# A recurrent mixing block: rel on GpSimd from an SBUF logarithm, nine hidden chunks on VectorE, the first sequence in halves, loads and all engine orders changed

## What is computed

```python
xn = layernorm(x)
shifted = pad(xn)[:, :-1]                       # one token later
k = (xn * mk + shifted * (1 - mk)) @ Wk         # v, r alike
r = sigmoid(r)
# for each token, per channel: num, den, mx carried on
out = (e1 * num + e2 * v) / (e1 * den + e2)     # with running maximum mx
s = (r * out) @ Wo
h = relu(xn @ w1[0] + b1[0])                    # 128 -> 512
z = layernorm(xn + h @ w2[0] + b2[0]) * gamma + beta
result = x + s * silu(z)
```

## Time and profile before

| | us |
|---|---|
| median of 3 runs | 112.2 (111.92 to 112.39) |
| span of the profiled execution | 110.7 |
| TensorE, VectorE, ScalarE, GpSimd busy in it | 101.9, 96.0, 94.3, 66.0 |

### The profile page before, as it was taken

The page is one execution under the profiler, slowest core; times in us unless marked ns, Lnnn a source line. Parts: engine busy times, 40 slices in busy tenths (PEclk is TensorE's granted clock), DMA queues, the critical chain, the costliest instruction groups (busy, mean ns, idle before and its releaser), DMA issues. The chain is left out here.

```text
span 110.7 us, 1604 instructions
## 1 busy us (share of the span) xinstructions
PE 101.9 (92%) x336; PEld 56.7 (51%) x336; DVE 96.0 (87%) x199; ACT 94.3 (85%) x155; POOL 66.0 (60%) x104
## 2 busy tenths in 40 slices
PE   4997799997999999999999999999999999999660
PEld 4993335553465445553675553674554566435230
DVE  1647989979999999799988989999999897899980
ACT  1425087899999998999899999999999999999940
POOL 3009998986746469459999998743819403360000
PEclk9999999999999999999999999999999999999998
DMA  3999200000000000000002110000000002203134
...
DMA packets 9450, 5.09 MB, mean 46 GB/s; under 512 B 481, under 2 KB 9185, under 8 KB 9441
## 3 DMA queue, kind: packets, MB, share of 16 engines
...
q10 hardware_dynamic: 560, 0.40, 1.3%
...
## 5 line engine op out<-in xcount | busy, mean ns | idle before, releaser
L638 PE MATMUL bank<-hid,w_c 128*128 128x512 f32 x64 | 31.1, 592 | 0.0
L589 PE MATMUL bank<-mixed,w_in 128*128 128x512 f32 x48 | 24.1, 599 | 0.8 <-POOL mixed L379 0.7
L475 ACT ACTIVATE hid<-bank,vec 128x512 f32<-128x512 f32 x32 | 21.4, 683 | 1.1 <-PE bank L611 0.7
L716 DVE SCALAR_TENSOR_TENSOR mixed<-step_x,vec,bank 128x511 f32<-128x511 f32 x24 | 17.5, 738 | 1.6 <-POOL step_x L370 1.6
L638 PEld LDWEIGHTS bank<-hid,w_c 128*128 128x128 f32 x64 | 11.9, 190 | 10.8 <-issue 9.3
L609 PE MATMUL bank<-xT_hi,w_hi 128*128 128x512 f32 x28 | 15.5, 552 | 1.1 <-POOL xT_lo L361 1.1
L589 PEld LDWEIGHTS bank<-mixed,w_in 128*128 128x128 f32 x48 | 8.4, 189 | 10.1 <-issue 8.6
L370 POOL TENSOR_TENSOR step_x<-xT 128x512 f32<-128x512 f32 x8 | 8.3, 1037 | 8.5 <-ACT xT L467 8.4
L403 POOL TENSOR_TENSOR dv<-v_sb 128x512 f32<-128x512 f32 x8 | 9.8, 1227 | 5.8 <-ACT v_sb L526 5.8
L340 POOL TENSOR_SCALAR xn<-x_sb,neg_mean,rstd 128x128 f32<-128x128 f32 x28 | 12.2, 449 | 0.0
L755 DVE TENSOR_TENSOR_SCAN dev<-keep,dv 128x512 f32<-128x512 f32 x8 | 9.8, 1220 | 1.7 <-issue 0.8
...
## 6 DMA issues: line engine op xcount, KB each, us to landing
x_sb<-x SPq DMA_DIRECT2D x7, 256.0 KB, 6.6
block_out<-res SPq DMA_DIRECT2D x7, 256.0 KB, 2.3
w_in<-squares SPq DMA_DIRECT2D x1, 256.0 KB, 3.0
w_in<-w ACTq DMA_DIRECT2D x1, 256.0 KB, 5.4
w_in<-w SPq DMA_DIRECT2D x1, 256.0 KB, 6.3
...
```

Source lines behind the costliest of these rows:

```text
L475: act.activation(hid[b % 2][:, f, :], ps(f"up{f}", b)[:, :], ACT.Relu, bias=vec[:, B1_COLUMN + f:B1_COLUMN + f + 1]).then_inc(done[f"hid{f ...
L589: pe.matmul(ps(name, b)[:, :], w_in[:, which, :], mixed[b % 2][:, which, :], start=True, stop=True).then_inc(done[name], 1)
L638: pe.matmul(ps("z", b)[:, :], w2_c[:, f, :], hid[b % 2][:, f, :], start=False, stop=chunks_of(b)[-1] == f"z{f}", skip_group_check=True).th ...
L716: dve.scalar_tensor_tensor(mixed[n][:, which, 1:], step_x[n][:, 1:], vec[:, which:which + 1], ps("z", b)[:, 0:T - 1], ALU.mult, ALU.add).t ...
```

## The change

- `rel` of all eight sequences moves from VectorE to GpSimd, which can't read PSUM; `ln_den` is therefore written to an SBUF tensor. `e_new` and `th_a` get SBUF tensors too, so bank `k` is freed by `gap`.
- Nine of the 32 `hid` steps move from ScalarE to VectorE (hid0 of 1, 3, 6; hid1 of 5, 6, 7; hid2 of 2; hid3 of 4, 5). `xT_hi` of sequences 1 and 6 moves to ScalarE, `d` of sequence 0 to VectorE.
- Sequence 0 is normalised, transposed, copied and sent through `up` in halves.
- SP loads w1 ahead of the squares, ScalarE loads x of sequence 1; the last half result is stored by ScalarE's queue.
- The waits are now worked out from the place of a step in the order of the engine that issues it; `norm1` counts once for each step instead of once for each tile.
- Warm-up has 7 and 2 calls; the order on all engines and the order of the banks are new (the banks' lists are left out below, and of the old orders all but the first and last lines).

```diff
-WARM_UP = 11
-KEEP_WARM = 4
+WARM_UP = 7
+KEEP_WARM = 2
...
 PROGRAM = {
     "pe": """
-        T:0 up3:0 b2m up2:0 k:0 T:1 up0:0 up1:0 v:0 k:1 up1:1 up0:1 up2:1 z0:0 z1:0 T:2 up3:1 z3:0 z2:0
...
-        z1:6 up3:7 up1:7 z0:6 z3:6 up0:7 back:2 var:6 v:6 s:4 up2:7 back:3 v:7 z0:7 back:4 z1:7 z2:7 r:6
-        r:7 z3:7 s:5 var.a:7 var.b:7 back:5 s:6 s.a:7 back:6 s.b:7 back.a:7 back.b:7
+        b2m T.a:0 T.b:0 up3.a:0 up0.a:0 up1.a:0 up2.a:0 up3.b:0 up0.b:0 up2.b:0 up1.b:0 v:0 T:1 k:0
+        z3:0 z1:0 z2:0 z0:0 k:1 T:2 var:0 up2:1 r:0 up1:1 up3:1 up0:1 z2:1 up1:2 z1:1 up3:2 z0:1
+        z3:1 k:2 up2:2 T:3 r:1 z1:2 z3:2 var:1 z2:2 up2:3 up1:3 v:1 up3:3 v:2 up0:2 up0:3 r:2 k:3
+        T:4 z0:3 z0:2 s:0 z3:3 var:2 T:5 z1:3 z2:3 up0:4 r:3 up1:4 v:3 var:3 up3:4 up2:4 k:4 k:5 T:6
+        z2:4 z1:4 up1:5 z3:4 s:1 z0:4 up3:5 back:0 v:4 z1:5 up0:5 var:4 up1:6 up2:5 T:7 s:2 up0:6
+        r:4 z2:5 up2:6 up3:6 v:5 z3:5 k:6 z0:5 r:5 v:6 k:7 z1:6 var:5 z3:6 z0:6 z2:6 up2:7 s:4 var:6
+        s:3 back:2 up1:7 z2:7 up3:7 back:1 v:7 up0:7 r:6 z1:7 z0:7 z3:7 r:7 back:3 s:5 var.b:7
+        var.a:7 back:4 s:6 s.b:7 back:5 back:6 s.a:7 back.b:7 back.a:7
     """,
     "act": """
-        ln_exp ve:0 rs:0 xT:0 neg_td w1_hi ve:1 rs:1 hid3:0 xT:1 hid0:0 hid2:0 wo hid1:0 v_sb:0 ve:2
...
-        v_sb:6 rstd2:6 ln_den:7 silu_set th_g:6 hid2:7 v_sb:7 th_a:6 th_g:7 th_a:7 silu:5 silu:6 th_r:6
-        th_r:7 sq.a:7 sq.b:7 ln_exp ln_var.a:7 ln_var.b:7 rstd2.a:7 rstd2.b:7 silu_set silu.a:7 silu.b:7
+        ln_exp ve.a:0 rs.a:0 ve.b:0 rs.b:0 neg_td w1_hi xT.a:0 xT.b:0 wo ve:1 rs:1 hid2:0 hid3:0
+        hid0:0 xT:1 hid1:0 xT_hi:1 ve:2 rs:2 v_sb:0 sq:0 e_new:0 xT:2 ln_var:0 e_keep:0 hid2:1
+        e_keep:1 e_new:1 hid1:1 ln_den:0 rstd2:0 hid3:1 ln_den:1 hid1:2 silu_set th_r:0 hid3:2
+        th_g:0 sq:1 th_a:1 xT:3 th_g:1 th_a:0 th_r:1 ln_exp ln_var:1 ve:4 rstd2:1 rs:4 hid2:3
+        e_new:2 e_keep:2 v_sb:1 hid3:3 hid1:3 ln_den:2 hid0:2 silu_set th_g:2 th_r:2 v_sb:2 xT:4
+        th_a:2 sq:2 silu:0 silu:1 ln_exp ln_var:2 xT:5 e_new:3 rstd2:2 e_keep:3 sq:3 hid0:4 hid1:4
+        v_sb:3 ln_var:3 rstd2:3 ln_den:3 hid2:4 silu_set th_g:3 silu:2 xT:6 th_a:3 th_r:3 ln_exp
+        e_new:4 e_new:5 e_keep:4 xT_hi:6 v_sb:4 sq:4 e_keep:5 hid0:5 ln_var:4 ln_den:4 rstd2:4
+        hid2:5 ln_den:5 xT:7 silu_set th_g:4 th_r:4 th_a:5 th_a:4 hid2:6 v_sb:5 th_g:5 hid3:6 silu:3
+        silu:4 th_r:5 sq:5 v_sb:6 ln_exp e_keep:6 e_new:6 ln_var:5 e_keep:7 rstd2:5 e_new:7 sq:6
+        hid2:7 ln_den:6 ln_var:6 ln_den:7 rstd2:6 silu_set th_g:6 hid3:7 th_a:6 v_sb:7 th_g:7 hid0:7
+        th_r:6 silu:6 th_a:7 silu:5 sq.a:7 sq.b:7 th_r:7 ln_exp ln_var.b:7 ln_var.a:7 rstd2.b:7
+        rstd2.a:7 silu_set silu.b:7 silu.a:7
     """,
     "dve": """
-        bnA:0 bnB:0 aggr1:0 norm1:0 bn:1 aggr1:1 ink:0 w2_sum cols bn:2 bn:3 aggr1:2 mx:0 inv:0 aggr1:3
...
-        inv:7 res:2 den:7 prod:4 rel:6 zn:6 res:3 rel:7 dev:6 adev:6 res:4 wkv:6 dev:7 gated:6 prod:5
-        adev:7 wkv:7 res:5 gated:7 prod:6 zn.a:7 zn.b:7 res:6 prod.a:7 prod.b:7 res.a:7 res.b:7
+        bn.a:0 aggr1.a:0 bn.b:0 aggr1.b:0 norm1.a:0 norm1.b:0 cols bn:1 aggr1:1 d:0 w2_sum inv:0
+        inr:0 ink:0 bn:3 bn:2 aggr1:3 aggr1:2 mx:0 ink:1 gap:0 inv:1 inr:1 mx:1 gap:1 bn:4 den:0
+        aggr1:4 bn:6 den:1 hid0:1 bn:7 zn:0 ink:2 inv:2 inr:2 bn:5 aggr1:7 mx:2 aggr1:6 gap:2 hid2:2
+        dev:0 aggr1:5 adev:0 inr:3 wkv:0 ink:3 gated:0 zn:1 den:2 inv:3 dev:1 hid0:3 adev:1 wkv:1
+        mx:3 gated:1 gap:3 dev:2 adev:2 inv:4 inr:4 wkv:2 gated:2 prod:0 zn:2 den:3 ink:4 ink:5
+        inv:5 hid3:4 zn:3 mx:4 inr:5 mx:5 gap:4 gap:5 hid1:5 dev:3 prod:1 adev:3 wkv:3 gated:3
+        hid3:5 res:0 den:4 den:5 hid1:6 ink:6 inv:6 prod:2 hid0:6 zn:4 inr:6 ink:7 dev:4 adev:4
+        wkv:4 mx:6 gap:6 gated:4 dev:5 mx:7 gap:7 adev:5 wkv:5 inv:7 den:6 den:7 zn:5 inr:7 gated:5
+        prod:4 zn:6 hid1:7 res:2 res:1 dev:6 adev:6 prod:3 wkv:6 dev:7 gated:6 adev:7 wkv:7 res:3
+        gated:7 prod:5 res:4 zn.b:7 prod:6 zn.a:7 res:5 prod.b:7 prod.a:7 res:6 res.b:7 res.a:7
     """,
     "pool": """
-        d:0 w1_lo nm:1 fix:0 norm1:1 w2_c d:1 xT_hi:1 fix:1 xT_lo:1 gmax:0 nm:2 gmin:0 norm1:2 gmin:1
...
-        gmin:5 gmax:5 xT_hi:7 dv:5 d:7 keep:5 fix:7 gmax:6 xT_lo:7 gmin:6 gmin:7 gmax:7 dv:6 keep:6 dv:7
-        keep:7
+        w1_lo nm:1 fix:0 norm1:1 w2_c d:1 fix:1 nm:2 norm1:2 gmin:0 xT_lo:1 gmax:0 gmax:1 gmin:1
+        xT_hi:2 xT_lo:2 d:2 rel:0 rel:1 fix:2 norm1:3 keep:0 dv:0 xT_hi:3 d:3 xT_lo:3 nm:4 gmax:2
+        gmin:2 keep:1 norm1:4 dv:1 fix:3 rel:2 norm1:5 keep:2 dv:2 xT_hi:4 d:4 xT_lo:4 fix:4 gmin:3
+        gmax:3 xT_hi:5 norm1:6 d:5 xT_lo:5 fix:5 dv:3 rel:3 norm1:7 keep:3 gmin:4 gmax:4 gmin:5
+        gmax:5 d:6 xT_lo:6 dv:4 rel:4 rel:5 d:7 fix:6 keep:4 dv:5 keep:5 fix:7 gmin:6 xT_hi:7 gmax:6
+        xT_lo:7 gmax:7 gmin:7 dv:6 rel:6 rel:7 keep:6 dv:7 keep:7
     """,
 }
...
-FREED_BY = {"z": ["zn"], "k": ["adev"], "v": ["v_sb", "wkv"], "r": ["gated"], "up0": ["hid0"], "up1": ["hid1"],
+FREED_BY = {"z": ["zn"], "k": ["gap"], "v": ["v_sb", "wkv"], "r": ["gated"], "up0": ["hid0"], "up1": ["hid1"],
...
+        e_new = pair("e_new", P, T)
...
+        ln_den = pair("ln_den", P, T)
...
+        th_a = pair("th_a", P, T)
...
+            if b < 0 or (b == 0 and step in NOT_FOR_FIRST):
+                return
+            if (step, half, b) in signal:
+                engine, count = signal[step, half, b]
+            elif half:
+                engine, count = signal[step, "", b]
+            else:
+                engine, count = max(signal[step, h, b] for h in "ab")
+            eng.wait_ge(done[engine, step], count)
...
             load_half(sp, 0)
+            sp.dma_start(w1_in[:, :], w1).then_inc(got["w1"], 16)
             sp.dma_start(w_in[:, :, :], squares).then_inc(got["squares"], 16)
-            load(sp, 1)
             sp.dma_start(w2_in[:, :, :], w2.rearrange("(f p) c -> p f c", p=P)).then_inc(got["w2"], 16)
             for b in range(2, B):
                 load(sp, b)
...
+            for b in range(LAST):
+                store(sp, b)
+            store(sp, LAST, "a")
...
+            def relative(b):
+                n = b % 2
+                after(pool, "gap", b)
+                after(pool, "ln_den", b)
+                after(pool, "th_g", b - 2)
+                after(pool, "th_a", b - 2)
+                pool.tensor_tensor(rel[n][:, :], gap[n][:, :], ln_den[n][:, :],
+                                   ALU.subtract).then_inc(done["pool", "rel"], 1)
...
             load_half(act, 1)
             act.dma_start(vec[:, :], vectors).then_inc(got["vec"], 16)
-            act.dma_start(w1_in[:, :], w1).then_inc(got["w1"], 16)
+            load(act, 1)
...
+            def evac_xT(b, half=""):
+                n, c = b % 2, cut(half)
+                if half == "a":
+                    act.wait_ge(prep["edges"], EDGES)
                 after(act, "T", b)
-                after(act, "d", b - 2)
-                after_split(act, "xT_hi", b - 2)
-                after_split(act, "xT_lo", b - 2)
+                for step in ("d", "xT_hi", "xT_lo"):
+                    after(act, step, b - 2)
                 if b == 2:
                     for f in range(NF):
                         after(act, f"up{f}", 0)
-                act.activation(xT[n][:, 1:], ps("z", b)[:, :], ACT.Copy).then_inc(done["xT"], 1)
+                act.activation(xT[n][:, 1 + c.start:1 + c.stop], ps("z", b)[:, c],
+                               ACT.Copy).then_inc(done["act", "xT"], 1)
+
+            def high_part(b):
+                n = b % 2
+                after(act, "xT", b)
+                for f in range(NF):
+                    after(act, f"up{f}", b - 2)
+                after(act, "xT_lo", b - 2)
+                act.activation(xT_hi[n][:, :], xT[n][:, 1:], ACT.Copy).then_inc(done["act", "xT_hi"], 1)
...
-                after(act, "gap", b)
-                act.activation(ps("k", b)[:, :], gap_min[b % 2][:, :], ACT.Exp, bias=neg_td[:, :]).then_inc(done["e_new"], 1)
+                after(act, "den", b - 2)
+                act.activation(e_new[b % 2][:, :], gap_min[b % 2][:, :], ACT.Exp,
+                               bias=neg_td[:, :]).then_inc(done["act", "e_new"], 1)
 
             def log_den(b):
                 after(act, "den", b)
-                act.activation(ps("k", b)[:, :], den[b % 2][:, 0:T], ACT.Ln).then_inc(done["ln_den"], 1)
+                after(act, "rel", b - 2)
+                act.activation(ln_den[b % 2][:, :], den[b % 2][:, 0:T], ACT.Ln).then_inc(done["act", "ln_den"], 1)
 
             def tanh_a(b):
                 after(act, "rel", b)
-                act.activation(ps("k", b)[:, :], rel[b % 2][:, :], ACT.Tanh, bias=half_neg_tf[:, :],
-                               scale=-0.5).then_inc(done["th_a"], 1)
+                after(act, "adev", b - 2)
+                act.activation(th_a[b % 2][:, :], rel[b % 2][:, :], ACT.Tanh, bias=half_neg_tf[:, :],
```

(97 more changed lines are left out.)

218 lines of the change are left out of this document (85 added, 133 removed).

## The result

The changed kernel takes 120.46 us (median, 119.36 to 121.93) against 112.15: 1.070 times as long, with an interval of 1.064 to 1.075. I forecast 109.9 us and a range up to 113.2; the measured time lies far outside, beyond the slowest of my rivals too (114.6). The profiled execution spans 118.5 us. Executions in a slower state of the chip are left out of every ratio in this document, but not of the medians.

The account below looks back on a forecast made before the run. TensorE and ScalarE set the pace, with VectorE becoming fullest. TensorE's 2.7 us lead plus 0.5 for the tail gave 108.5 us, VectorE's work, holes and last store 108.4; adding 1.5 us span-to-median gave 109.9, range 107.4 to 113.2.

Parts of the forecast that it names:

- its holes: VectorE's idle time after 7.5 us, taken as 4.2 us: 1.5 from the walk, 0.8 in the tail, 1.9 between.
- The sum: VectorE's time: 101.7 us without holes, 105.9 with 4.2 of holes, then 2.5 for the last store: 108.4 span.
- VectorE's work behind 7.5 us: VectorE's busy time after 7.5 us: 97.4 in all less 3.2 done before, 94.2 us.
- The row: Earlier trace: GpSimd's xT_hi took 1.33 us at 66.95 while VectorE's scan dev ran from 66.65 to 67.88.
- GpSimd is late: Rival: VectorE's reads hold GpSimd, making TensorE wait over 2.7 us; 2.4 us slower, 114.6 us, chance 0.10.
- GpSimd's load: GpSimd's busy time: 72 us after the moved steps, 77 to 80 with 5 to 8 us of holding.
- the 24 writes: e_new, ln_den and th_a written to SBUF instead of PSUM: costed at nothing, bounded at 1 us either way.
- the mixing step's end of my bound: Nine hid chunks on VectorE at 0.60 us each, or 0.66 if they cost as a mixing step.
- the rest of the walk: Start followed step by step: first up at 7.15 us, v:0 10.9, up2:1 18.75; lead 3.5 us, later 2.7.
- The clock: Fewer warm-up passes may slow TensorE's first products, 3.4 us at worst; part of the lead-given-back rival, chance 0.14.
- The tail: VectorE's queue from the second last batch's table load: 13.9 us against 12.1, so 1.8 longer, inside VectorE's sum.

## Why the prediction was wrong

- **Which engine sets the pace: right.** I named VectorE the fullest and gave its holes 4.2 us; they are 4.7. The sum 7.5 + 103.8 + 4.7 + 2.5 = 118.5 is the prediction's own. It closes because the stretch ends where VectorE ends; what it tells is which term moved: the holes by 0.5 us, the work by 9.6. Being full did not make VectorE the cause of everything: GpSimd was equally full till 50 us.
- **The term that failed: VectorE's work behind 7.5 us, 94.2 forecast, 103.8 measured.** I read the earlier trace rows as "GpSimd is held during the read" and charged the 16 new reads to GpSimd alone; on VectorE I put their waiting at nothing. The runs show that VectorE waits as well: den, dev and adev together 10.5 us, and sums over one SBUF tensor in the place of den and adev give back 6.8 us of time. The row showed a case in which VectorE had come first, and the trace of before has no other: dev took 1194 to 1227 ns in all eight, but each time it began when GpSimd stood idle, most often just after the keep or dv that dev waits for (keep ends at 66.57, dev starts at 66.65). Four times GpSimd began an instruction during dev, and it was that one which lasted longer (fix 0.70 us for 0.30, xT_hi 1.33 for 0.61, two dv 1.87 and 1.72 for 1.04). den and adev are not released by GpSimd (den waits for e_new and e_keep, adev for th_a and dev), and so can begin in the middle of its work. My rival "GpSimd is late" had the shared cause but only one of its two victims, at 114.6 us with a chance of 0.10.
- **GpSimd's load.** 82.4 us against 77 to 80. I priced rel at 1.04 by d, which reads the same tensor twice; xT_lo, with two tensors, was at 1.27 and the nearer row. rel took 1.29, 2.0 us more in all. My estimate of GpSimd's own holding from this: 66.0 + 10.3 - 2.2 = 74.1, so 8.3 us, at the end of the 5 to 8 that I charged.
- **ScalarE's outputs in SBUF: right.** I bounded the 24 writes at 1 us; e_new lasts 718 ns (692 before), ln_den 624 (602), th_a 713 (685), 0.6 us in all.
- **hid on VectorE.** 0.65 start to start, not 0.60: the mixing step's end of my bound. This is 0.5 us.
- **The start.** First up at 7.04 (7.15 forecast), transposes done at 6.42 (6.4). But x of sequence 1 let bn:1 start at 8.84: I took 7.5 and had 9.3 as the other end. v:0 began at 12.05, not 10.9, and up2:1 at 20.14, not 18.75. With x on time they began at 10.80 and 18.88, so the rest of the walk was right. Priced by experiment: about 1 us (0.8 to 1.5).
- **The clock.** Fewer warm-up passes did no harm at the start: the eight half products took 3.69 us, from 7 to 11 us at a granted clock of 1.00 (the 2.4 GHz level). Later TensorE stood idle from 54.0 to 56.58 us, waiting for wkv behind the stretched dev; from 56.5 to 61 its granted clock was 0.63, so partly at the 1.2 GHz level. What this cost was not measured.
- **The tail.** I had VectorE's queue longer by 1.8 us, but not that the last stores come close together: SP issues five of them from 109.06 us on. The last res waits 1.10 us for the store of res:5, whose buffer it reuses:

```profile
115.24 0.76 DVE L870 TENSOR_TENSOR res<-bank,x_sb 128x256 f32<-128x256 f32 x2 [1.10 <-DMA block_out<-res]
```
